# Spreading the reciprocal deviation and the shift over the channels through DRAM rows, in a metaformer layer on one core

## What is computed

```python
y  = _ln_c(x)                       # per position: (x - mean over channels) / sqrt(var + 1e-6)
theta, phi = cbr(y, th_w), cbr(y, ph_w)            # 32 channels each; cbr = relu(scale * (W y) + shift)
Gs = einsum('bci,bcj->bij', theta, phi)            # 784 x 784, never stored by the kernel
joint = cbr(concat([Gs^T, Gs]), ggs_w)             # 196 rows
gate  = sigmoid(bn(ws2 . cbr(concat([mean(cbr(y, gxs_w)), joint]), ws1_w)))
x1 = gate * y                                      # gate over positions
# the same over channels: theta_c, phi_c, Gc (128 x 128), ggc, gxc, wc1, wc2
x2 = x + sigmoid(W_yc) * x1
t  = tokens of x2;  z = _ln_t(t)                   # per token, eps 1e-5
p  = softmax(z @ router_w + router_b); the two best of 8 experts, weights normed to 1
out = t + sum over the two of p * (z @ expert_w[e] + expert_b[e])
```

## Time and profile before

| | |
|---|---|
| median of three runs | 2032.25 us (2031.36 to 2032.88) |
| the profiled execution | 2032.81 us, its span 2031.0 us |
| busy: PE, DVE, ACT, POOL | 1923.5, 1467.5, 1127.4, 1049.6 us |
| mean granted clock of TensorE | 0.989 |
| DMA | 57.72 MB, mean 28 GB/s |

### The profile page before, as it was taken

The page is one execution under the profiler, slowest core; times in us unless marked ns, Lnnn a source line. Parts: engine busy times, 40 slices in busy tenths (PEclk is TensorE's granted clock), DMA queues, the critical chain, the costliest instruction groups (busy, mean ns, idle before and its releaser), DMA issues.

```text
span 2031.0 us, 40647 instructions
## 1 busy us (share of the span) xinstructions
PE 1923.5 (95%) x14196; PEld 1438.2 (71%) x14196; DVE 1467.5 (72%) x4761; ACT 1127.4 (56%) x3176; POOL 1049.6 (52%) x1169
## 2 busy tenths in 40 slices
PE   1689999999999999999999999999999999999996
PEld 1467777777777777777777777777777777777774
DVE  1347878777787777777877778787777777777776
ACT  1345555665555556555565655556565555565543
POOL 0134565564456555455555545655644565554555
PEclk9799999999999999999999999999999999999998
DMA  3000000000000000000000000000000000000000
GB/s 105 1 17 17 33 17 33 33 25 25 33 29 22 33 25 30 27 33 17 33 33 25 25 33 33 17 33 33 25 25 33 33 17 33 25 33 25 17 17 32
DMA packets 23702, 57.72 MB, mean 28 GB/s; under 512 B 5132, under 2 KB 6333, under 8 KB 23502
## 3 DMA queue, kind: packets, MB, share of 16 engines
q1 hardware_dynamic: 23502, 55.13, 7.8%
HBM read 29.43 MB, written 25.69 MB: 27 GB/s over the span
## 4 chain that ended last, share of the span: by engine, by line
PE 59%; DVE 25%; issue 9%; ACT 4%; POOL 2%; SPq 1%; DMA 0%; DVEq 0%; POOLq 0%; ACTq 0%
DVE part L1449 8%; PE low L1046 4%; PE rot L861 4%; PE rot L841 4%; PE high L1046 4%; ACT part L643 3%; PE low L1048 3%; PE low L1047 3%; DVE eq L1392 3%; PE rot L874 3%; PE high L1048 3%; DVE tok L1319 2%; PE high L1047 2%; PE rot L788 2%; PE rot L780 2%
## 5 line engine op out<-in xcount | busy, mean ns | idle before, releaser
L643 ACT ACTIVATE part<-low,gv 128x128 f32<-128x128 f32 (+1 forms) x1664 | 458.4, 391 | 214.1 <-issue 109.2
L446 POOL TENSOR_TENSOR part<-part 128x256 f32<-128x256 f32 (+1 forms) x416 | 328.6, 790 | 435.2 <-DVE part L1449 435.2
L1449 DVE SCALAR_TENSOR_TENSOR part<-high,gv,part 128x128 f32<-128x128 f32 (+1 forms) x1664 | 457.9, 341 | 121.4 <-PE high L1048 108.5
L905 PE MATMUL rot<-x1h,wch 112*128 112x256 f32 x1120 | 280.5, 287 | 3.7 <-ACT tok L514 3.7
L906 PE MATMUL rot<-x1h,wcl 112*128 112x256 f32 x1120 | 274.3, 282 | 0.0
L451 POOL TENSOR_TENSOR otok<-part 128x128 f32<-128x128 f32 (+1 forms) x416 | 241.7, 581 | 32.6
L408 POOL TENSOR_TENSOR rstd<-var,mhalf 112x14 f32<-112x14 f32 x32 | 85.2, 2662 | 274.2 <-DVE var L1247 274.2
L905 PEld LDWEIGHTS rot<-x1h,wch 112*128 112x128 f32 x1120 | 212.7, 190 | 9.1 <-ACT tok L514 4.3
L906 PEld LDWEIGHTS rot<-x1h,wcl 112*128 112x128 f32 x1120 | 212.7, 190 | 0.1
L1046 PE MATMUL low<-weh,xh 128*128 128x512 f32 (+1 forms) x416 | 188.3, 453 | 15.5 <-ACT part L643 12.6
L1046 PE MATMUL high<-weh,xh 128*128 128x512 f32 (+1 forms) x416 | 188.2, 452 | 2.5 <-DVE part L1449 2.5
(11 more groups left out here) (207 smaller groups left out, 3821.7 us busy)
## 6 DMA issues: line engine op xcount, KB each, us to landing
xin<-in_x SPq DMA_DIRECT2D x32, 784.0 KB, 4.3
out<-x SPq DMA_DIRECT2D x64, 392.0 KB, 2.3
otok<-in_ggs_w SPq DMA_DIRECT2D x1, 600.2 KB
y_ch<-in_ggs_w SPq DMA_DIRECT2D x1, 600.2 KB
j<-in_expert_w SPq DMA_DIRECT2D x1, 512.0 KB
x<-in_thc_w SPq DMA_DIRECT2D x1, 392.0 KB
x<-in_phc_w SPq DMA_DIRECT2D x1, 392.0 KB
x<-in_gxc_w SPq DMA_DIRECT2D x2, 183.8 KB
```

What stands on the lines that cost most here:

```text
L446: nc.gpsimd.tensor_tensor(part[0:n, slot, 0:2, :], part[0:n, slot, 0:2, :], part[0:n, slot, 2:4, :], ALU.add).then_inc(sem("half_sum"), 1)
L643: last = nc.scalar.activation(part[0:n, turn % RING, e, :], low[turn % 2][0:n, e * C:(e + 1) * C], ACT.Copy, scale=gv[par(p, back)][0:n, i ...
L905: nc.tensor.matmul(dst, wch[:, j, rows], hi_x, start=(j == 0), stop=False)
L1449: last = nc.vector.scalar_tensor_tensor(out=own, in0=high[turn % 2][0:n, e * C:(e + 1) * C], scalar=gv[par(p, back)][0:n, i, HALF + e:HALF ...
```

## The change

- `scale` and `shifts` are gone. `rstd_turn` and `shift_turn` make one transpose each, of the whole 112 x 14 or 128 x 13 tile. ScalarE copies the rows to SBUF, SP writes them to a DRAM tensor of the kernel's own, waits for that DMA, and reads the rows back, each of the 128 partitions the same 1568 numbers, into `y_ch` or `cen`. `normalise` and `centre` then work in place, with both operands in SBUF.
- x is read twice: once into a single buffer `xin`, from which tokens and `normalise` read, and once into `x2`, where `residual` adds in place.
- The token tile has three sets (`third`) for two.
- The weights are in three lists: `small` and `expert` go on SP's queue, `wide` (the channel weights and what belongs to them) on ScalarE's, each list with a semaphore of its own, and TensorE waits for each scaled channel weight by itself.
- The lists of all engines and the table `USES` are in a new order; a step now spans `back` 0 to 5, and `DEPTH` is 6. The new list of ScalarE goes: space_exp(3), theta_phi(0,2), tp_high(0,2), gx(0,2), tp_tokens(0,2), gate_low(7,5), gx(1,2), gate_low(8) and (9), x1_high(0,3), gate_low(10,5), the four x_tokens(1), shift_copy(4), x1_high(1,3), theta_phi(1,2), tp_high(1,2), gate_low(11) and (12), tp_tokens(1,2), channels(0,3), mix_copy, mix_high(2), the four x_high(4), channels(1,3), joint(0,0) of both images(2), logit_copy(4), gram_copy(0,3), channels(2,3), gram_copy(1,3), router_exp(4), joint_c(3), rstd_copy(1), joint(0,1)(2), hidden_c(3), gate_low(0) to (2)(4), joint(1,0)(2), channel_exp(3), gate_low(3) to (6)(4), joint(1,1)(2), hidden(0) and (1)(2), space_copy(2). That of GpSimd: tp_low(0,2), inverse_std2(4), x1_low(0) and (1)(3), add_token(7) to (10)(5), tp_low(1,2), add_token(11) and (12)(5), inverse_std1(1), the four x_low(4), add_token(0) to (6)(4).

The diff without those two lists, the table, and VectorE's old list (indentation cut by eight):

```diff
-x = [sb(f"xin{p}", [C, PAIR, S]) for p in range(2)]
+xin = sb("xin", [C, PAIR, S])
...
+both_rows = sb("both_rows", [64, 128])
+rstd_row, shift_row = both_rows[0:2 * NT, 0:T], both_rows[32:32 + TILES, :]
+rows_dram = {name: nc.dram_tensor(f"{name}_rows", (2, n, w), F32, kind="Internal").ap()
+             for name, n, w in (("rstd", 2 * NT, T), ("shift", TILES, 128),)}
...
+def third(k, p, back):
+
+    return (2 * k + p - back) % 3
...
+expert = [
+    (raw_we, a["expert_w"].rearrange("e d c -> d e c")),
+    (raw_eb, a["expert_b"].rearrange("(o e) c -> o (e c)", o=1)),
+    (raw_wr[:, :], a["router_w"]), (raw_rb[:, :], a["router_b"].rearrange("(o n) -> o n", o=1)),
+]
+
+wide = [
     (raw_ggc[:, :], a["ggc_w"]), (raw_sggc[:, :], col(a["ggc_s"])), (bggc[0:IC, :], col(a["ggc_b"])),
     (bggc[IC:2 * IC, :], col(a["ggc_b"])),
...
 for m, r, w, lo, hi in stack:
-    small += [(rawc_all[m][r:r + hi - lo, :], a[w + "_w"][lo:hi, :]),
-              (raw_sc[r:r + hi - lo, m:m + 1], col(a[w + "_s"][lo:hi])),
-              (bc[r:r + hi - lo, m:m + 1], col(a[w + "_b"][lo:hi]))]
-
-def load_x(eng, k, p, back):
+    big.append((rawc_all[m][r:r + hi - lo, :], a[w + "_w"][lo:hi, :]))
+    wide += [(raw_sc[r:r + hi - lo, m:m + 1], col(a[w + "_s"][lo:hi])),
+             (bc[r:r + hi - lo, m:m + 1], col(a[w + "_b"][lo:hi]))]
+wide = big + wide
...
 @block.sync
 def _(sp):
-    load_x(sp, 0, 0, 0)
+    load_x(sp, xin, "x_loaded", 0, 0, 0)
     sp.wait_ge(sem("zeroed"), 7)
     for dst, src in small:
         sp.dma_start(dst, src).then_inc(sem("weights_loaded"), 16)
-    load_x(sp, 0, 1, 0)
+    for dst, src in expert:
+        sp.dma_start(dst, src).then_inc(sem("expert_loaded"), 16)
...
         def load(back):
-            if live(k, p, back) and live(k, p, back + 2):
-                need(sp, "x2_ready", k, p, 4, back + 2)
-                load_x(sp, k, p, back)
+            if live(k, p, back) and live(k, p, back + 1):
+                need(sp, "y_ch_ready", k, p, 4, back + 1)
+                need(sp, "x_tok_filled", k, p, 4, back + 1)
+                load_x(sp, xin, "x_loaded", k, p, back)
+
+        def load_residual(back):
+            if live(k, p, back):
+                o = par(p, back)
+                if live(k, p, back + 2):
+                    sp.wait_ge(sem(f"stored{o}"), (k + (p - back - o) // 2) * (16 * PAIR))
+                else:
+                    sp.wait_ge(sem("prep_filled"), 2 * NT + 2 * MT)
+                load_x(sp, x2[o], "x2_loaded", k, p, back)
...
+        def row_out(name, src, back):
+            if live(k, p, back):
+                need(sp, f"{name}_row_ready", k, p, 1, back)
+                sp.dma_start(rows_dram[name][turn(back) % 2], src[:, :]).then_inc(sem(f"{name}_row_out"), 16)
+
+        def row_in(name, dst, back):
+            if live(k, p, back):
+                sp.wait_ge(sem(f"{name}_row_out"), 16 * (turn(back) + 1))
+                sp.dma_start(dst, rows_dram[name][turn(back) % 2].rearrange("i t -> (i t)")[0:PAIR * S].partition_broadcast(128))\
+                  .then_inc(sem(f"{name}_spread"), 16)
+
+        def rstd_out(back):
+            row_out("rstd", rstd_row, back)
+
+        def rstd_in(back):
+            if live(k, p, back):
+                need(sp, "tp_filled", k, p, 2, back + 1)
+                need(sp, "gx_filled", k, p, 2, back + 1)
+                row_in("rstd", y_ch[:, :, :].rearrange("p b s -> p (b s)"), back)
+
+        def shift_out(back):
+            row_out("shift", shift_row, back)
+
+        def shift_in(back):
+            if live(k, p, back):
+                need(sp, "xl_ready", k, p, 4, back + 1)
+                need(sp, "logit_filled", k, p, 1, back + 1)
+                row_in("shift", cen[:, :, :].rearrange("p b s -> p (b s)"), back)
+
+        shift_out(4)
+        shift_in(4)
+        store(0, 5)
+        store(1, 5)
+        load_residual(3)
+        rstd_out(1)
+        rstd_in(1)
         load(0)
-        store(0, 3)
-        store(1, 3)
 
     steps(sp, step)
...
 def _(act):
 
+    act.wait_ge(sem("zeroed"), 7)
+    for dst, src in wide:
+        act.dma_start(dst, src).then_inc(sem("wide_loaded"), 16)
...
+        def rstd_copy(back):
+            if live(k, p, back):
+                if live(k, p, back + 1):
+                    act.wait_ge(sem("rstd_row_out"), 16 * (2 * k + p - back))
+                need(act, "rstd_row_filled", k, p, 1, back)
+                nc.scalar.copy(rstd_row[:, :], bank("rstd_row", k, p, back)[0:2 * NT, 0:T]).then_inc(sem("rstd_row_ready"), 1)
...
     for m in range(MT):
+        pe.wait_ge(sem("wide_scaled"), m + 1)
         for j0, j1_ in QUART:
...
                 if (b, q) == (0, 0):
-                    pe.wait_ge(sem(f"x_loaded{o}"), (k + (p - back - o) // 2) * 16 + 16)
+                    pe.wait_ge(sem("x_loaded"), 16 * (2 * k + p - back + 1))
                 free(pe, f"x_tok{b}{q}", k, p)
-                to_tokens(f"x_tok{b}{q}", x[o], b, q, back).then_inc(sem("x_tok_filled"), 1)
-
-        def scale(b, q, back):
-            if live(k, p, back):
-                free(pe, f"scale{b}{q}", k, p)
+                to_tokens(f"x_tok{b}{q}", xin, b, q, back).then_inc(sem("x_tok_filled"), 1)
+
+        def rstd_turn(back):
+            if live(k, p, back):
+                free(pe, "rstd_row", k, p)
                 need(pe, "rstd1_ready", k, p, 1, back)
-                spread(f"scale{b}{q}", rstd1[par(p, back)], b, q, back).then_inc(sem("scale_filled"), 1)
+                nc.tensor.transpose(bank("rstd_row", k, p, back)[0:2 * NT, 0:T], rstd1[par(p, back)][:, :], ident[0:T, 0:T])\
+                    .then_inc(sem("rstd_row_filled"), 1)
 
...
-        def shifts(f, back):
-            if live(k, p, back):
-                free(pe, f"shift{f}", k, p)
+        def shift_turn(back):
+            if live(k, p, back):
+                free(pe, "shift_row", k, p)
                 need(pe, "shift_ready", k, p, 1, back)
-                for i in range(*FLAT[f]):
-                    n = rows(i)
-                    last = nc.tensor.transpose(bank(f"shift{f}", k, p, back)[:, (i - FLAT[f][0]) * 128:][:, 0:n],
-                                               shift[0:n, i:i + 1].to_broadcast([n, 128]), ident[0:n, 0:n])
-                last.then_inc(sem("shift_filled"), 1)
+                nc.tensor.transpose(bank("shift_row", k, p, back)[0:TILES, 0:128], shift[:, :], ident[:, :])\
+                    .then_inc(sem("shift_row_filled"), 1)
...
-        x2_tokens(0, 2)
-        x2_tokens(1, 2)
-        joint(0, 0, 1)
-        low_half(7, 3)
-        low_half(8, 3)
-        x2_tokens(2, 2)
-        x2_tokens(3, 2)
-        joint(0, 1, 1)
-        finish(1, 3)
-        low_half(9, 3)
-        low_half(10, 3)
-        hidden(0, 1)
-        low_half(11, 3)
-        joint(1, 0, 1)
-        joint(1, 1, 1)
-        high_half(6, 3)
-        shifts(0, 2)
-        shifts(1, 2)
-        shifts(2, 2)
-        hidden(1, 1)
-        high_half(7, 3)
-        high_half(8, 3)
-        space_logit(1)
-        shifts(3, 2)
-        high_half(9, 3)
-        low_half(12, 3)
-        space_turn(1)
-        high_half(10, 3)
-        logits(2)
-        x_tokens(0, 0, 0)
-        x_tokens(0, 1, 0)
-        x_tokens(1, 0, 0)
-        x_tokens(1, 1, 0)
-        high_half(11, 3)
-        high_half(12, 3)
-        low_half(0, 2)
-        router(2)
-        low_half(1, 2)
-        finish(2, 3)
-        high_half(0, 2)
-        channels0_high(1)
-        high_half(1, 2)
-        channels0_low(1)
-        finish(3, 3)
-        channels(1, 1)
-        low_half(2, 2)
-        low_half(3, 2)
-        gram_first(1)
-        channels(2, 1)
-        scale(0, 0, 0)
-        scale(0, 1, 0)
-        gram_turn(1)
-        high_half(2, 2)
-        high_half(3, 2)
-        joint_c(1)
-        scale(1, 0, 0)
-        scale(1, 1, 0)
-        low_half(4, 2)
-        hidden_c(1)
-        finish(0, 2)
-        theta_phi(0, 0)
-        theta_phi(1, 0)
-        channel_logit(1)
-        high_half(4, 2)
-        high_half(5, 2)
-        tp_tokens(0, 0)
-        tp_tokens(1, 0)
-        gx(0, 0)
-        gx(1, 0)
-        mixed(0)
-        x1_channels(0, 0, 1)
-        x1_channels(0, 1, 1)
-        x1_channels(1, 0, 1)
-        x1_channels(1, 1, 1)
-        low_half(5, 2)
-        low_half(6, 2)
+        space_turn(3)
+        finish(0, 5)
+        finish(1, 5)
+        theta_phi(0, 2)
+        x2_tokens(2, 4)
+        x2_tokens(3, 4)
+        gx(0, 2)
+        tp_tokens(0, 2)
+        low_half(7, 5)
+        gx(1, 2)
+        low_half(8, 5)
+        high_half(8, 5)
+        low_half(9, 5)
+        x_tokens(0, 0, 1)
+        x_tokens(0, 1, 1)
+        x_tokens(1, 0, 1)
+        x_tokens(1, 1, 1)
+        low_half(10, 5)
+        high_half(9, 5)
+        low_half(11, 5)
+        high_half(10, 5)
+        low_half(12, 5)
+        shift_turn(4)
+        theta_phi(1, 2)
+        high_half(11, 5)
+        high_half(12, 5)
+        channels0_high(3)
+        tp_tokens(1, 2)
```

(121 more changed lines are left out.)

373 lines of the change are left out of this document (163 added, 210 removed).

## The result

The changed kernel takes 1959.06 us (median of 4 runs, 1957.01 to 1962.08), against 2032.56 us (2031.36 to 2032.88) for the kernel before on the same chip: ratio 0.9641, 95% interval 0.9624 to 0.9657. It is 3.6% faster. The prediction said 1916 us with a range of 1888 to 1985: the sign and the range held, the value was 43 us too low.

The account below looks back on a forecast made before the run. TensorE was taken to bound the kernel, busy 395.8 of 400 us. Sum: 2032.8 - 87 (spreads) - 26 (order) - 18 (weights) + 12 (fill) + 2 (drain) = 1915.8, about 1916 us; range 1888 to 1985.

Parts of the forecast that it names:

- Spreads off TensorE: On TensorE, one transpose of each kind replaces 14 for rstd and 13 for shift: -2.7 us a turn, -87 us.
- New order: TensorE's reordered work: fewer runs of halves and small waits gone, less 0.4 us for dense gates; -0.8 us a turn, -26 us.
- The two small waits above: TensorE's waits for the low part of x1 and a ScalarE gate, 0.5 us a turn, claimed to vanish.
- 7 x 0.10: On TensorE, expert halves in 9 runs a turn instead of 16, 0.10 us saved per run: 0.7 us a turn.
- VectorE and GpSimd: SBUF operand locks slow centre and normalise, but VectorE's idle time and cover absorb it: 0 us, bounded by +1.
- Rival (b): Dense stretch of gates or locks between VectorE and GpSimd cost 2 us a turn: +64, 1980 us; chance 14%.
- Trips through DRAM: Shift and rstd rows via DRAM take 7.4 us a trip, covered by other work in the turn: 0 us.
- (a): Rstd trip outlasts its cover, 11 to 13.5 us; each us past 10.6 costs one a turn; 1961 us at 12; chance 14%.
- (c): 128 reads of one row served one after another; slower than before from a 14.2 us trip, 2217 us at 20; chance 7%.
- Weights: Weight loads split over two queues, landed at about 24, start the first turn earlier: -18 us, at least 11 from scaling order.
- Fill: First turn's chain with an uncovered trip and reordered work, plus one stage more to fill: +12 us (6 to 20).
- Drain: At the end, one more uncovered shift trip against a better mixed order of last halves: +2 us (-6 to +12).

Follow-up runs that it names:

- e1: Changed kernel with the single row transposes made 14 and 13 times over, restoring TensorE's old amount of small transposes; 2029.58 us.
- b3: Changed kernel with shifts before the second token product, first image load behind the weights, and three TensorE groups fewer a turn; 1944.15 us.
- e5: Changed kernel with six more awaited writes of the rstd row to DRAM before the one that counts; 2137.21 us.
- e6: Changed kernel with six more awaited writes of the shift row to DRAM before the one that counts; 2129.65 us.
- e4: Changed kernel with three more awaited writes of the rstd row to DRAM before the one that counts; 1977.78 us.

## Why the prediction was right in sign and 43 us low

Against the profiled execution, 1957.0, the miss is 41 us. By the three intervals, with the forecast's -3.5 a turn counted in all 32 of them: start +6.3 instead of -6, turns -76.8 instead of -113, end -5.2 instead of +2. That is +12, +36 and -7, together 41. The +36 is, about, 17 for the order, 13 for the spreads, and the rest for the last turns and the 32nd that the forecast counted.

- **Spreads off TensorE, -2.7 us a turn: right in kind, 0.4 too good.** From start to start the two kinds took 3.02 us of an old turn and take 0.40 of a new one, -2.62. A single transpose here holds TensorE 0.20 us, not the 0.07 that I took from a pair. e1 shows that the kernel gains 2.3 us of it.
- **New order, -0.8 us a turn: the step that failed.** It is worth 0.3 us (e1). Two things were mis-sized. First, "The two small waits above, 0.5 us, also have a place in the new order where nothing is late": they went, but 0.67 us for the shift came. Second, the 7 x 0.10 for fewer runs of halves. The halves did get cheaper, from 20.53 us in 16 runs to 19.9 in 9 (20.57 less the wait for the shift that is in it), and the channel products fell by 0.7; but 0.17 and 0.35 us of these two are the old waits for the gate and the low part of x1, which lay in them and are not to be counted twice. But the new order splits other groups: the transposes of x1 in three runs for one (+0.3), residual projections and mixed products +0.25, gram and joints +0.3. I counted the runs of one kind and not of all; and b3 says that a price per run does not add up anyway.
- **VectorE and GpSimd, 0, bounded by +1: the missed 0.67 us.** The lock was in the rows and in the argument, but priced for the eight instructions that change to SBUF operands. It hit one that had them already, 13 numbers wide, which the new order puts next to GpSimd's subtraction. Rival (b) had the mechanism at three times the size; the dense stretch of gates, its other half, cost nothing (TensorE waited 1.4 us for gates in 26 turns).
- **Trips through DRAM, 0 in a turn: right.** 5.3 us from the write for the first one (61.33 to 66.60), and 6.1 and 5.5 in the median, against 7.4. VectorE has 4.4 us to spare for rstd, where the forecast had 1.5 there and 3 in all, and 5.3 for the shift, where it had 3.5 there and 6 in all. Rivals (a) and (c) fall: the repeated address costs nothing. The price behind the cover was wrong: (a) and (c) took one for one, and e5 and e6 show 1.1 and 1.6 us of period for each us of VectorE's wait. The prediction's 5.8 us from the Trainium skill (DMA: Bandwidth & Descriptors, Anatomy of one DMA) comes near the 5.5 and 6.1, but the page gives its fit for DMAs that GpSimd issues, and these are issued by SP.
- **Weights, -18: -12.5.** Near the lower bound of 11, but for another reason, so by luck. That bound took the loads as no earlier and gave the whole gain to the order of the scaling. In fact the list landed 8.95 us earlier, at 26.65 and not at "about 24", and the order gave only 3.5: the transposes of the channel weights start 8.65 us behind VectorE's first scaling (35.30), where it was 12.2 before, and the prediction had 0.7. It overlooked the transposes of the joint weights, which stand ahead on TensorE from 30.83 to 35.30. The 15.1 us behind them stayed, 15.0. The prediction's own sign for this, a first turn near 50, is what came.
- **Fill, +12: +18.8**, inside its bound of 20. The first chain up to the space logits' turn takes 42.9 us instead of 35.9. The prediction counted one uncovered rstd trip in it; there are three before the first gate value, with 19.3 us of waits of VectorE. e4 and e5 say the same: 4.6 and 8.9 us more a trip move the first gate value by 12.5 and 27.7 us, about three times as much. What the deeper pipeline adds beside this was not taken apart.
- **Drain, +2: about -5** after the last gate value, near the good bound of -6. Why was not looked into.
